# Two sorted expert stages: router products and zeroed rows moved into the stages ahead, gathers on four semaphores

## What is computed

```python
# moe2: router, the two best of 8 experts, each a two-layer MLP 128 -> 512 -> 128
logits = jnp.einsum('bsd,ed->bse', x, gate_w)
probs = jax.nn.softmax(logits, axis=-1)
topk_probs, topk_idx = jax.lax.top_k(probs, 2)
oh = jax.nn.one_hot(topk_idx, 8, dtype=x.dtype)
h = jax.nn.gelu(jnp.einsum('bsd,fed,bske->bskf', x, w1, oh) + jnp.take(b1, topk_idx, axis=0))
y = jnp.einsum('bskf,def,bske->bskd', h, w2, oh) + jnp.take(b2, topk_idx, axis=0)
out = jnp.sum(y * topk_probs[..., None], axis=-2)
```

## Time and profile before

| | us |
|---|---|
| median of 3 runs (lowest, highest) | 3646.87 (3643.24, 3654.44) |
| the profiled execution | 3638.4, span 3636.6 |
| PE busy | 2888.4 (79%) |
| DVE busy | 2171.3 (60%) |
| ACT busy | 1921.8 (53%) |
| POOL busy | 1485.3 (41%) |
| gathers, line 897: idle of GpSimd before them, all 128 | 167.4 |
| scatters, line 889: idle of GpSimd before them, all 128 | 152.2 |

### The profile page before, as it was taken

The page is one execution under the profiler, slowest core; times in us unless marked ns, Lnnn a source line. Parts: engine busy times, 40 slices in busy tenths (PEclk is TensorE's granted clock), DMA queues, the critical chain, the costliest instruction groups (busy, mean ns, idle before and its releaser), DMA issues. The chain is left out here.

```text
span 3636.6 us, 57509 instructions
## 1 busy us (share of the span) xinstructions
PE 2888.4 (79%) x17312; PEld 1918.3 (53%) x17377; DVE 2171.3 (60%) x5654; ACT 1921.8 (53%) x4572; POOL 1485.3 (41%) x1443
## 2 busy tenths in 40 slices
PE   6759996679845789999989959999649468497898
PEld 2216773458843445555555625555449424354676
DVE  6747884640245677666788736767412468796343
ACT  4546662525635168777887737777236346111232
POOL 1002220216240298777888724444263433365000
PEclk9979997779977689999999979999679779799899
DMA  3540002134831010000000014444458322000000
GB/s 66 84 80 1 12 6 82 47 108 148 226 103 35 27 42 14 19 17 16 19 14 19 11 47 122 123 122 122 129 161 229 105 64 79 11 1 1 25 0 23
DMA packets 198732, 232.64 MB, mean 64 GB/s; under 512 B 26481, under 2 KB 161378, under 8 KB 198114
## 3 DMA queue, kind: packets, MB, share of 16 engines
q1 hardware_dynamic: 183778, 206.70, 20.6%
q0 software_dynamic: 8192, 16.79, 1.5%
q10 hardware_dynamic: 6528, 6.29, 1.3%
HBM read 165.26 MB, written 40.36 MB: 57 GB/s over the span
## 5 line engine op out<-in xcount | busy, mean ns | idle before, releaser
L2980 POOL TENSOR_TENSOR local_size<-local_size,local_half_powers 128x8 f32<-128x8 f32 x128 | 257.9, 2015 | 18.8 <-issue 0.2
L2691 PE MATMUL bank<-local_wqkv,local_shifted 128*128 128x512 f32 x384 | 217.1, 650 | 14.2 <-DMA local_shifted<-normed_t 11.1
L855 ACT ACTIVATE moe_hid<-bank,moe_record 128x128 f32<-128x128 f32 x640 | 182.9, 369 | 82.7 <-PE bank L762 82.1
L1597 POOL TENSOR_TENSOR ssm_decay<-ssm_decay,ssm_future 128x1024 f32<-128x1024 f32 x64 | 137.6, 2151 | 212.4 <-DMA ssm_decay<-ssm_sums_of 212.4
L1077 DVE TENSOR_TENSOR moe_outs<-bank,moe_record 128x128 f32<-128x128 f32 x160 | 46.0, 291 | 298.2 <-PE bank L775 295.9
L119 POOL TENSOR_TENSOR branch_norm_shifted<-branch_norm_moments,eps 128x4 f32<-128x4 f32 x48 | 9.6, 201 | 474.1 <-DVE branch_norm_moments L112 473.8
L4076 POOL TENSOR_TENSOR rwkv_added<-rwkv_values_of,rwkv_rows_of 128x256 f32<-128x256 f32 x128 | 80.3, 627 | 284.7 <-PE bank L4051 203.8
L897 POOL DMA_INDIRECT moe_found<-moe_sorted_outs,moe_slots x128 | 122.1, 954 | 167.4 <-DMA moe_sorted_outs<-moe_outs 89.3
L2869 ACT ACTIVATE local_probs<-bank,local_peak 128x128 f32<-128x128 f32 x512 | 184.5, 400 | 5.0 <-issue 2.6
L889 POOL DMA_INDIRECT moe_sorted_rows<-normed,moe_slots x128 | 123.4, 964 | 152.2 <-DMA moe_sorted_rows<-normed,moe_slots 77.9
L775 PE MATMUL bank<-moe_seconds,moe_hid 128*128 x1280 | 176.3, 282 | 2.5 <-ACT moe_hid L855 1.4
(11 more groups left out here) (595 smaller groups left out, 8279.5 us busy)
## 6 DMA issues: line engine op xcount, KB each, us to landing
moe_record<-in_moe_records_dram SPq DMA_DIRECT2D x160, 322.0 KB, 3.5
ssm_decay<-ssm_sums_of SPq DMA_DIRECT2D x64, 768.0 KB, 4.9
mamba_decay<-mamba_sums_of SPq DMA_DIRECT2D x16, 768.0 KB
moe_sorted_rows<-moe_found SPq DMA_DIRECT2D x20, 512.0 KB, 6.6
moe_rows_in<-moe_sorted_rows SPq DMA_DIRECT2D x80, 128.0 KB, 3.4
moe_sorted_outs<-moe_outs SPq DMA_DIRECT2D x80, 128.0 KB, 3.7
local_across<-local_values SPq DMA_DIRECT2D x64, 128.0 KB, 2.3
rwkv_kept<-rwkv_keep SPq DMA_DIRECT2D x8, 768.0 KB, 15.6
```

The source lines that it names most:

```text
L855: last = act.activation(hid[:, k % 2, f, :], hbank[k % 2][:, f * UNIT:(f + 1) * UNIT], ACT.Gelu_apprx_tanh, bias=record[:, k, B1 + f:B1 + ...
L1597: pool.tensor_tensor(diagonal, diagonal, future[:].unsqueeze(1).unsqueeze(1).broadcast_to([P, QUAD, 2, P]), ALU.add).then_inc(masked, 1)
L2691: pe.matmul(bank[:], shifted[:, at, t * P:(t + 1) * P], wqkv[:, of // 2 // PAIRS, part * INNER:(part + 1) * INNER], start=True, stop=True) ...
L2980: pool.tensor_tensor(part, part, half_powers[:], ALU.pow).then_inc(scaled, 1)
```

## The change

The 32 router products of moe0 are made at the end of rwkv_out and those of moe2 at the end of ssm, into a bank of PSUM that is free there and stays untouched until VectorE reads it in the next stage. In rwkv_out the first seven pairs' products stand ahead of the last turn and the last pair's after it; in ssm two pairs' stand ahead of the sums, five ahead of the last turn, one after it. The router's weights are loaded in those stages, and VectorE waits at their end for the last product. The arrays of sorted rows are shared by both expert stages and written with zeros once, by ten copies from an array of zeros in DRAM, two behind each gate load of the first five pairs in rwkv_out; SyncE waits for all at the end of it. A gather waits for the gather four before it, not two, on four semaphores.

```diff
 UNIT = P
 GROUP = 8
+MOE0_PARTS = MOE2_PARTS = (4, 4)
+
+def router_products(core, pe, bank, router, i):
+    for t in range(i * PT, (i + 1) * PT):
+        last = pe.matmul(bank[:, t * EXPERTS:(t + 1) * EXPERTS], core.normed_t[:, t * P:(t + 1) * P], router[:],
+                         start=True, stop=True)
+    return last
+
-def sorted_moe(core, name, tail, parts, shared, normalised):
+def sorted_moe(core, name, tail, parts, shared, normalised, rows_dram, logits_bank):
...
-        rows_dram, outs_dram = [[nc.dram_tensor(f"{name}_sorted_{n}{p}", (groups_of[p] * GROUP * P, C), F32,
-                                                kind="Internal").ap() for p in PARTS] for n in ("rows", "outs")]
+        outs_dram = [nc.dram_tensor(f"{name}_sorted_outs{p}", (groups_of[p] * GROUP * P, C), F32,
+                                    kind="Internal").ap() for p in PARTS]
...
-        found_in = [sem(f"found_in{k}") for k in range(2)]
+        found_in = [sem(f"found_in{k}") for k in range(4)]
...
         @block.sync
         def _(sp):
-            sp.dma_start(router[:], dram[f"{name}_router"]).then_inc(router_in, 16)
...
-            sp.wait_ge(blank_ready, 1)
-            for p in PARTS:
-                for g in range(groups_of[p]):
-                    sp.dma_start(rows_dram[p][g * GROUP * P:(g + 1) * GROUP * P, :].rearrange("(k p) c -> p k c", p=P),
-                                 blank).then_inc(blanked, 16)
...
         @block.tensor
         def _(pe):
-            pe.wait_ge(router_in, 16 * router_loads)
-            for t in range(TILES):
-                last = pe.matmul(lbank[:, t * EXPERTS:(t + 1) * EXPERTS], core.normed_t[:, t * P:(t + 1) * P], router[:],
-                                 start=True, stop=True)
-            last.then_inc(logits_up, 1)
...
             def scale_first(i):
-                act.wait_ge(found_in[0], 16 * PT * (i + 1))
-                act.wait_ge(found_in[1], 16 * PT * (i + 1))
+                for quarter in found_in:
+                    act.wait_ge(quarter, 16 * (PT // 2) * (i + 1))
...
         @block.gpsimd
         def _(pool):
-            pool.memset(blank, 0.0)
-            pool.drain()
-            pool.sem_inc(blank_ready, 1)
             pool.wait_ge(slots_ready, 1)
-            pool.wait_ge(blanked, 16 * ALL_GROUPS)
...
                 for n in rows:
                     k, t = n % 2, i * PT + n // 2
-                    if t > 0:
-                        pool.wait_ge(found_in[k], 16 * t)
+                    before = i * (PT // 2) + n // 4
+                    if before > 0:
+                        pool.wait_ge(found_in[n % 4], 16 * before)
                     pool.indirect_dma_start(found[:, k, t, :], None, outs_dram[part_of_pair[i]][:, :],
                                             bass.IndirectOffsetOnAxis(ap=slots[:, k, t:t + 1], axis=0)
-                                            ).then_inc(found_in[k], 16)
+                                            ).then_inc(found_in[n % 4], 16)
...
-            dve.wait_ge(logits_up, 1)
-            raw = lbank[:, 0:TILES * EXPERTS].rearrange("p (t e) -> p t e", e=EXPERTS)
+            raw = logits_bank[:, 0:TILES * EXPERTS].rearrange("p (t e) -> p t e", e=EXPERTS)
...
-def ssm_block(core, tail):
+def ssm_block(core, tail, logits_bank):
...
             sp.dma_start(future[:], dram["future"]).then_inc(weights_in, 16)
+            sp.dma_start(router[:], dram["moe2_router"]).then_inc(weights_in, 16)
...
+            def route(i):
+                pe.wait_ge(fresh_stored, i + 1)
+                return router_products(core, pe, logits_bank, router, i)
+
             mix_octet(ALL // EACH - 1)
-            for at in behind:
-                item(*at)
+            for i in range(2):
+                route(i)
+            item(*behind[0])
+            item(*behind[1])
+            for i in range(2, PAIRS - 1):
+                route(i)
+            item(*behind[2])
+            route(PAIRS - 1).then_inc(logits_up, 1)
...
             fresh(PAIRS - 1)
+            dve.wait_ge(logits_up, 1)
...
-def rwkv_out(core, tail, heads, kept, mixed_out, x_back):
+def rwkv_out(core, tail, heads, kept, mixed_out, x_back, rows_dram, logits_bank):
...
+        blanks = [rows[at:at + GROUP * P, :] for rows in rows_dram for at in range(0, rows.shape[0], GROUP * P)]
...
+            sp.dma_start(router[:], dram["moe0_router"]).then_inc(weights_in, 16)
...
                 sp.dma_start(gate[:], kept[i, :, 1:3, :]).then_inc(gate_in, 16)
+                for rows in blanks[2 * i:2 * i + 2]:
+                    sp.dma_start(rows, dram["zeros"]).then_inc(blanked, 16)
+            sp.wait_ge(blanked, 16 * len(blanks))
...
-            pe.wait_ge(weights_in, 64)
+            pe.wait_ge(weights_in, 80)
...
             tail.pe(pe, PAIRS - 2)
+            pe.wait_ge(relu_done, PAIRS * HC)
+            for i in range(PAIRS - 1):
+                pe.wait_ge(tail.turned_stored, i + 1)
+                router_products(core, pe, logits_bank, router, i)
             tail.pe(pe, PAIRS - 1)
+            pe.wait_ge(tail.turned_stored, PAIRS)
+            router_products(core, pe, logits_bank, router, PAIRS - 1).then_inc(logits_up, 1)
...
             tail.dve_fresh(dve, PAIRS - 1)
+            dve.wait_ge(logits_up, 1)
...
+        rows_dram = [nc.dram_tensor(f"sorted_rows{p}", (n * GROUP * P, C), F32, kind="Internal").ap()
+                     for p, n in enumerate(groups)]
...
+        "zeros": np.zeros((GROUP * P, C), np.float32),
```

36 lines of the change are left out of this document (20 added, 16 removed).

## The result

The changed kernel takes 3598.6 us at the median (3596.7 to 3604.3) where the kernel before takes 3645.1 (3638.4 to 3654.4). The ratio of the runs is 0.9877, with an interval of 0.986 to 0.9893. That is 45 us less, between 39 and 51. The profiled execution has a span of 3597.3 against 3636.6.

What follows compares the result with a forecast made beforehand. The kernel was taken as bound by stages in a row with barriers between, so only the chain ending a stage counts. The terms sum to -35.5 us, from a median of 3646.9 to 3611, range 3594 to 3629.

Steps and rivals of the forecast that it cites:

- Head of moe2, -14.8: Start of moe2: VectorE reads the logits right after its memset, and the chain to the first unit moves 14.8 us earlier.
- Head of moe0, -11.5: Start of moe0: TensorE begins the dense expert when its weights land, so the dense chain starts 11.5 us earlier.
- Ends of the stages ahead, +1.8 each: Ends of rwkv_out and ssm: the last pair's four products follow ScalarE's store and hold the barrier, 1.8 us each.
- The other 28 tiles, +0.5: Remaining router products in TensorE's waits: +0.3 us in rwkv_out, overrunning as the clock falls, and +0.2 in ssm.
- Router loads, +0.9: Starts of ssm and rwkv_out: the router loads add an issue on SyncE's queue, 0.9 us together.
- Zeros, 0 (bounds 0 and +5): Ten zero copies in rwkv_out fit within 15 us per two; removing the old stores is worth nothing by itself.
- The rival on the slower side: Zero copies block SyncE's queue in rwkv_out, 3811 us if one engine carries each; decides from 22 us for two; chance 0.05.
- Gathers in the tails, -8.7: Ends of moe0 and moe2: waits between gathers shrink to the queue's 0.3 us gap, saving 4.7 and 4.0.
- the pace is not set by the semaphore: Rival: GpSimd's transfers are worked off one behind the other, so 14.2 us of gain goes, giving 3625; chance 0.15.
- Gathers between the units, -6.0: Both expert stages: ScalarE's waits before scaling shrink by 5.2 us at the first pairs and 0.8 at the other three.
- +0.5 for the further waits: Both expert stages: ScalarE waits on four semaphores in place of two, 32 more waits, 0.5 us (bounds 0 and 9.6).
- All of it counts: Rival: the four pairs between units win 12 us and stage ends cost 0.9 each: -43.5, 3603; chance 0.10.

Runs made afterwards that it cites:

- Experiment 3: The changed kernel with the zeros stored at the heads of both expert stages as before; 1.0091 on the second chip, where the kernel before takes 3711.1 us.
- second profile of before: The kernel before run again with no edit, on a chip like the first; 1.0008 of itself.
- experiment 10: The changed kernel with six copies of zeros behind each of the first five gate loads in place of two; 0.9885 of the kernel before.
- experiment 6: The changed kernel with its gathers back on two semaphores, on a chip like the first; 3622.1 us, 0.9916 of the kernel before.
- experiment 8: The changed kernel with the gathers between units half a pair earlier in GpSimd's order; 3593.3 us, 0.9842 of the kernel before.
- experiment 2: The changed kernel with its gathers back on two semaphores, on the second chip; 0.9931 of the kernel before.

## Why the prediction was right, step by step

The mechanism forecast for the heads and the tails is the one that the profiles show. Two things in the number are luck: the zeros in the head of moe2 were moved without being priced, and two misses in the tails go opposite ways.

**Head of moe2, -14.8.** Measured -15.0 (63.7 against 78.7). The chain moved as one piece, and the tables were in time. But the working had a hole: it called the missing stores "worth nothing by itself", and they would have become the last comer. Experiment 3 shows it: with the stores left where they were, 9.5 of the 15.0 are lost again. The sum came out since both edits were made; the credit belongs to both. The trace of before had the number: the ten stores ended some 26 after the stage began, the slots came at 31.7 and were to come at 16.9.

**Head of moe0, -11.5.** Measured -12.0; `own` landed 4.2 after the stage's start, where 4 to 5 were named, and the dense chain still ends last (its last result at 82.8, the rows' load at 73.8).

**Ends of the stages ahead, +1.8 each.** Measured +2.2 each. The four tiles took their 1.87, and the barrier after them opens a little later than after ScalarE's store. In the stage of ssm as a whole it does not show: 462.2, before 462.8 and 463.0. Some of it came back just ahead: from VectorE's last gating of ssm to its first use of the output product 6.15 passed in the changed kernel (2566.86 to 2573.01) and 7.13 in the first profile of before, since the clock stood at 2.4 GHz for longer (two us into the sums of squares it was 1.00 in the changed kernel, 0.50 before). That is no gain of the change: this stretch took 5.7 in the second profile of before and 7.2 in experiment 10.

**The other 28 tiles, +0.5.** Measured 0. In ssm the sums start 3.25 after the product ahead of them, before 3.23, and the 20 tiles behind took 8.5 and left 1.7 (forecast 8.6 and 1.4). In rwkv_out the step was wrong, though its size was small: I took the moment at which the clock fell in before, where TensorE had been idle from 757.1 on, for the moment in the changed kernel, where it works. Windows of the changed kernel:

```profile
757.00:759.00 2.00, 2.00 (x20) 2.00 (x20) 1.53 (x9) 0.60 (x1) 0.20 (x1) 1.00 0.00 0
759.00:761.00 2.00, 2.00 (x21) 2.00 (x20) 0.82 (x4) 0.00 (x0) 1.01 (x1) 1.00 0.00 0
761.00:763.00 2.00, 2.00 (x18) 2.00 (x18) 1.85 (x7) 0.00 (x0) 0.00 (x0) 0.87 0.00 0
```

All 56 instructions ran at 2.4 GHz or nearly so, in 6.8. In ssm it went the other way: the first two pairs' products ran at 1.00, the clock fell in the output product behind them (between 2571 and 2573), though TensorE had work all the time, and the 20 tiles from 2572.76 on ran at 0.50 (the same profile):

```profile
2568.00:2571.00 3.00, 3.00 (x28) 3.00 (x29) 0.00 (x0) 0.54 (x2) 0.20 (x1) 1.00 0.02 5
2571.00:2574.00 3.00, 3.00 (x20) 3.00 (x18) 0.99 (x4) 0.00 (x0) 1.21 (x2) 0.59 0.01 3
2574.00:2577.00 3.00, 3.00 (x16) 3.00 (x15) 1.38 (x9) 0.00 (x0) 1.21 (x2) 0.50 0.00 0
```

The Trainium skill ("TensorE: Matmul & The Clock Gate", Part 1), by which activity releases the gate, gave about 6 and hidden for rwkv_out, nearer than my row; the windows of ssm, where the clock went while the engine was busy, don't agree with it.

**Router loads, +0.9.** The first arrays of rwkv_out are issued 0.8 later against the stage's start (5.51, before 4.70), of which 0.35 is a slower first issue. As forecast.

**Zeros, 0 (bounds 0 and +5).** Measured 0: VectorE's joins from the third pair on have no idle time before them, in the kernel before, in the changed one and in experiment 10; the stage as a whole varies by up to 3. Two copies landed 4.7 to 7.0 after their issue, under the 9 that were named, and six of them do no harm either. The rival on the slower side, a copy carried by one engine at 27 each, has no case here. The point from which it decides was not reached with six copies of 512 KB.

**Gathers in the tails, -8.7.** Measured -3.8 and -4.8 against before, -3.5 and -4.7 by experiment 6. The rival "the pace is not set by the semaphore" falls: the waits of the earlier trace rows are gone to the last. The sum fits better than its parts: 4.7 was forecast for moe0 and 3.5 to 3.8 measured, 4.0 for moe2 and 4.7 to 4.8 measured. In moe0 the gathers gained 5.6 and the tail 3.8, for there the norms are next. PE's turns of the last pairs come 10.6 apart, behind VectorE, while the gathers need 10.0 a pair:

```profile
1073.28 1.11 PE L212 MATMUL bank<-ident,fresh 128*128 128x128 f32 x4 [9.49 <-DVE fresh L140]
...
1083.89 1.12 PE L212 MATMUL bank<-ident,fresh 128*128 128x128 f32 x4 [9.50 <-DVE fresh L140]
```

**Gathers between the units, -6.0, and +0.5 for the further waits.** This term was too small by some 3. The two stretches in sum are 378.2, 371.6 and 373.6 with two semaphores, 363.2 and 368.7 with four (after and experiment 10): 8.5 on the means. ScalarE's waits in front of its scaling say the same: 23.5, 19.5 and 20.0 against 12.3 and 13.0, 8.3 on the means. Those of the first pair (5.2, 3.7 and 5.0) went whole. At the other three pairs I had 0.8; there it is 18.3, 15.8 and 15.0 against 12.3 and 13.0, so some 3.7 went. I had argued that half of their gathers are queued behind a power. That is true of the 12.3, which experiment 8 took away by that very order, but I passed over the landings themselves. Those of before's gathers between the units of moe0, by their line:

```profile
DMA to landing us min/median/max: 2.5/3.5/5.8
```

Against 2.5 in the tail, a landing of 3.5 with two in flight makes a pace of 1.75 or more by estimate, so there was more to win for GpSimd than in the tails; how much of it reaches ScalarE the rows of before do not say. The extra waits of ScalarE cost nothing that shows.

**The sum.** By these: -15.0 - 12.0 + 4.4 + 0.9 - 8.2 to -8.6 - 8.5 = -38 to -39, where -35.5 stood; the ratio of the runs says -45, between -39 and -51. By whole stages it comes nearer. On the means of the two profiles of before and of after with experiment 10 (198.3, 327.6, 465.3 and 300.0 there), rwkv_out is 1.5 longer, moe0 20.5 shorter, ssm 0.8 longer and moe2 25.3 shorter: -43.5. The stages ahead grew by 2.3 in all, less than the 5.3 counted at their ends and starts, and the head of moe2 in the second profile of before was 2.6 longer. The rest lies within what the profiles of one kernel vary by. "All of it counts" (3603) was the nearest of the named cases.

**What the prediction had no case for** is the second chip. A kernel that is 1.2% faster on one chip is 0.7% slower on another, by something that no row of the first trace shows: there TensorE went through the scatters at its full pace.

## What to carry to other kernels

When two edits each free the same event, price each with the other undone: the second last comer is in the trace, and here it was worth two thirds of the gain in the head of moe2. Waits on indirect transfers can be relieved by more semaphores up to the queue's own pace, and then the order of the queue is the next thing to look at (the gathers half a pair earlier gave 11 more). A result from one chip is a result for chips like it: an engine's idle time put down to "issue" for tens of us, beside an unbroken run of indirect transfers, is the sign to look for. And a load that is late by the clock is to be counted by the work of the engine that asks for it before it is called the cause.

## What was not expected of the hardware

- On one chip, TensorE and VectorE went slowly while GpSimd's indirect transfers ran back to back: TensorE at 41 matmuls in 60 us, with no load of instructions from 830 to 890, VectorE with 2.4 to 5.2 idle before each step in a tail; outside such runs, and in the tails with gathers 1.41 apart, all went as on the first chip. Loads did get through between scatters 0.30 apart (experiment 2 at 888.8). The Trainium skill ("Runtime: NRT & Kernel Launch", Instruction fetch mechanics) has each engine fetch its instructions in 16 KB blocks over a DMA queue of its own, mostly hidden. The first profile agrees (a load of 0.02 MB on queue 8 in the midst of the scatters, with TensorE at its full pace). Whether the slow pace on the second chip has to do with the fetch, no run here shows.
- Copies of 512 KB from DRAM to DRAM landed after 4.7 to 7.0 two at a time and up to 9.9 six at a time.
- The clock stood at 2.4 GHz through the router products from 757 to 761 in rwkv_out, and fell to 1.2 at the end of ssm, between the first two pairs' products and the others, with TensorE busy in both.
- A pause until all indirect transfers are landed costs 1.8 to 2.4, not the 1.0 to 1.3 between landing and pace.
